# One attention and mixture-of-experts kernel on one core: VectorE's small work moved between its masking operations, both engines on the even unit's copy, value projections moved into the first two row tiles

## The reference

```python
xn = layernorm(x)
q, k, v = (xn @ W).reshape(4096, 2, 64)  for Wq, Wk, Wv
scores = einsum('nhd,mhd->hnm', q / 8, k)          # 2 heads, 4096 x 4096 each
scores = where(adj > 0, scores, -9e15)
attn = softmax(scores, axis=-1)
sat = einsum('hnm,mhd->nhd', attn, v).reshape(4096, 128)
y = concat([sat[:2048] @ weightr, sat[2048:] @ weightd]) + bias
x = x + leaky_relu(y, 0.01)
z = layernorm(x)
# 8 experts, top 2 chosen by gate scores; the mask is 0 or 1
h = gelu(einsum('td,edh->teh', z, W1) + b1)        # 256 hidden values each
x = x + sum over the chosen experts of (h @ W2 + b2)
```

## Time and profile before

| what | value |
|---|---|
| median of 3 runs | 851.81 us |
| profiled execution: time, and its span | 851.31 us, 849.5 us |
| PE busy | 811.7 us, 96% of the span |
| ACT busy | 679.0 us, 80% |
| DVE busy | 639.2 us, 75% |
| POOL busy | 195.5 us, 23% |
| chain that ended last | PE 73%, POOL 14%, issue 8%, DVE 3% |
| preparation, until the first scores | 0 to 41.2 us |
| step 0 and 1, until step 2's first transposes | 41.2 to 74.3 us |
| step 2 to the last scores | 74.3 to 633.7 us |
| last transposes and products, until the experts start | 633.7 to 657.5 us |
| feed-forward | 657.5 to 849.5 us |

### The profile page before, as it was taken

One profiled execution on the slowest core, in us unless ns is written; L12 is line 12 of the kernel. 1 busy time (PEld: TensorE's weight loads), 2 busy tenths in 40 slices (PEclk: granted clock), 3 DMA queues, 4 the chain that ended last, 5 costly groups with the idle time before them and its releaser, 6 DMA issues.

```text
span 849.5 us, 31821 instructions
## 1 busy us (share of the span) xinstructions
PE 811.7 (96%) x12080; PEld 597.7 (70%) x12080; DVE 639.2 (75%) x1530; ACT 679.0 (80%) x1099; POOL 195.5 (23%) x209
## 2 busy tenths in 40 slices
PE   4969999999999999999999999999997889999997
PEld 2537777777777777777777777777776567777775
DVE  6597888888888888888888888887883465555555
ACT  4838887878788888878888888788885789999996
POOL 4180000100100010000001000000000566766774
PEclk9979999999999999999999999999999999999999
DMA  8515433443343334434333443443100000000000
GB/s 220 110 25 91 81 58 58 66 74 58 56 77 59 56 61 72 65 56 69 67 56 58 68 71 56 63 72 56 31 0 2 1 14 14 14 14 12 12 12 12
DMA packets 40900, 44.96 MB, mean 53 GB/s; under 512 B 22168, under 2 KB 32160, under 8 KB 40864
## 3 DMA queue, kind: packets, MB, share of 16 engines
q0 software_dynamic: 9216, 33.56, 24.6%
q1 hardware_dynamic: 31216, 10.71, 5.4%
q10 hardware_dynamic: 432, 0.20, 0.1%
HBM read 71.72 MB, written 2.10 MB: 87 GB/s over the span
## 4 chain that ended last, share of the span: by engine, by line
PE 73%; POOL 14%; issue 8%; DVE 3%; DMA 1%; ACT 0%; POOLq 0%; DVEq 0%
PE ps L912 28%; PE ps L881 19%; PE ps L896 19%; POOL prob L349 14%; PE ps L923 2%; PE ps L837 1%; PE ps L842 1%; PE ps L850 1%; DVE prob L589 1%; PE ps L931 1%; PE ps L828 1%; DMA x_sb<-in_x 1%; DVE stats L513 0%; POOLq L348 0%; ACT prob L418 0%
## 5 line engine op out<-in xcount | busy, mean ns | idle before, releaser
L589 DVE CUSTOM_DVE_ANT_0 prob<-ps,mask 128x1024 f32<-128x1024 f32 x256 | 311.8, 1219 | 90.1 <-PE ps L881 84.4
L418 ACT ACTIVATE prob<-prob,nmax 128x1024 f32<-128x1024 f32 x256 | 292.8, 1144 | 9.9 <-DVE nmax L597 9.9
L912 PE MATMUL ps<-pt,v_sb 128*64 128x128 f32 x4096 | 253.2, 277 | 0.0
L912 PEld LDWEIGHTS ps<-pt,v_sb 128*64 128x64 f32 x4096 | 222.4, 137 | 13.4 <-issue 7.5
L433 ACT ACTIVATE pt<-ps 128x1024 f32<-128x1024 f32 x128 | 131.1, 1024 | 113.0 <-PE ps L896 113.0
L896 PEld LDWEIGHTS ps<-ident,prob 64*128 64x128 f32 x4096 | 152.6, 139 | 78.5 <-issue 78.4
L881 PE MATMUL ps<-k_half,q_row 64*128 64x512 f16 x1536 | 189.7, 380 | 5.0 <-DVE low L589 5.0
L896 PE MATMUL ps<-ident,prob 64*128 64x64 f32 x4096 | 183.7, 229 | 9.4 <-issue 4.7
L349 POOL TENSOR_TENSOR prob<-prob 128x512 f16<-128x512 f32 x104 | 122.6, 1183 | 57.1 <-ACT prob L483 54.4
L294 POOL DMA_DIRECT2D mask<-in_adj x64 | 35.4, 553 | 429.2 <-DVE low L589 429.2
L791 DVE SCALAR_TENSOR_TENSOR x_sb<-ps,k_half,x_sb 128x128 f32 (+1 forms) x256 | 72.5, 344 | 78.1 <-PE ps L1029 76.8
(11 more groups left out here) (97 smaller groups left out, 670.8 us busy)
## 6 DMA issues: line engine op xcount, KB each, us to landing
mask<-in_adj POOLq DMA_DIRECT2D x64, 512.0 KB, 5.5
q_row<-q_nat SPq DMA_DIRECT2D x128, 32.0 KB, 4.7
x_sb<-in_x SPq DMA_DIRECT2D x4, 512.0 KB, 7.0
out<-x_sb SPq DMA_DIRECT2D x8, 256.0 KB, 2.3
pt<-in_L_ffn_W SPq DMA_DIRECT2D x1, 1024.0 KB, 6.5
wq_sb<-in_L_gnn_Wq ACTq DMA_DIRECT2D x1, 64.0 KB, 2.9
wk_sb<-in_L_gnn_Wk ACTq DMA_DIRECT2D x1, 64.0 KB, 4.5
wv_sb<-in_L_gnn_Wv ACTq DMA_DIRECT2D x1, 64.0 KB, 5.7
```

The costliest lines, as they stand in the source:

```text
L418: act.activation(prob[:, h, cols], prob[:, h, cols], ACT.Exp, bias=nmax[:, h:h + 1], scale=-1.0, accum_out=sums[:, j, h, p:p + 1]).then_in ...
L589: dve.tensor_tensor_reduce(out=prob[:, h, col_of(p)], in0=ps[:, 2 * (u % 2):2 * (u % 2) + 2, :].rearrange("p b c -> p (b c)"), in1=mask[:, ...
L912: ins = pe.matmul(ps[dims, AV, 0:P], v_sb[:, tile, dims], pt[:, UNITS.index((h, p)), t, :], start=(tile == 0), stop=(tile == NT - 1))
```

## The change

It has these parts:

- **Copies:** ACT and DVE now empty one bank each for the even units (2k), and ACT alone empties both for the odd units (2k+1). `copies_by_dve` counts accordingly.
- **DVE's order:** small work that stood behind the odd mask of a quarter now stands between the even mask and the odd mask; `finish_tile` goes ahead of unit 2's copy; `residual` moves from the odd step into the next even one; `keep_logits` into the next odd step. The odd mask now waits for the transposes by itself (it stood behind the copy that did).
- **PE's order:** `x2_transpose` and `logits` go behind the quarter's `attend`.
- **Value projections:** all eight leave the preparation. Five run in step 0, between its scores, three in step 1. `xn_t` is no ring any more: it holds all eight chunks in units 4 to 7 of `pt`. The expert weights are loaded into `x2t_hi` and `x2t_lo` instead of there.
- **POOL's order:** the loads of `adj` for tiles 2 and 3 now come ahead of the splitting of the weights, which no longer waits for `k_lo_ready`.
- **Tail:** `rank_gates` moves from ahead of the last step into it, behind unit 2's copy. Steps 4 and 5 are now written out too.

```diff
-        w1_raw = pt[:, 4:6, :, :].rearrange("p u k q -> p (u k q)")
-        w2_raw = pt[:, 6:8, :, :].rearrange("p u k q -> p (u k q)")
+        w1_raw = x2t_hi[:, :].bitcast(F32)
+        w2_raw = x2t_lo[:, :].bitcast(F32)
...
-        xn_t = area(0, 4, 4).rearrange("p (r c) -> p r c", r=4)
+        xn_t = pt[:, 4:NU, :, :].rearrange("p u k q -> p (u k q)").rearrange("p (j c) -> p j c", j=NC)
...
-            return NU // 2 * j + units // 2
+            return NU // 2 * j + (units + 1) // 2
...
             load_adj(1, 1)
-            pool.wait_ge(k_lo_ready, NC)
+            load_adj(2, 0)
+            load_adj(3, 1)
             pool.wait_ge(w1_in, 16)
             split_weights(0, w1_raw, w1_pair)
...
-            for i in range(2, 6):
-                load_adj(i, i % 2)
+            load_adj(4, 0)
+            load_adj(5, 1)
...
-                copy_v(2 * p)
-                copy_v(2 * p + 1)
...
+            for j in range(V_FIRST):
+                copy_v(j)
...
-                if u % 2:
+                if u % 2 == 0:
                     act.activation(pt[:, u, :, 0:DH], ps[:, TR0, :].rearrange("p (k q) -> p k q", k=KT),
                                    ACT.Copy).then_inc(pt_by_act, 1)
...
+                    if early and u in (1, 3, 5):
+                        copy_v(V_FIRST + u // 2)
...
+                if u % 2 and prior:
+                    dve.wait_ge(transposed, NU * i - NU + u + 1)
...
                 for u in range(NU):
-                    if prior and u % 2:
+                    if finish and u == 2:
+                        finish_tile(i - 2, par)
+                    if prior and u % 2 == 0:
                         copy_pt(i - 1, u, early)
                     if now:
-                        mask_scores(i, par, u)
+                        mask_scores(i, par, u, prior)
                         if u in (5, 7):
                             row_max(i, u // 7, u)
-                    if u == 1 and finish:
-                        finish_tile(i - 2, par)
-                    if ahead and u in (3, 7):
+                    if ahead and u in (2, 6):
                         make_mask(i + 1, 1 - par, u // 4)
                     if post and par == 1:
-                        if u == 1:
+                        if u == 0 and ready:
+                            keep_logits(i - 5)
+                        if u == 0:
                             invert_sums(i - 3)
-                        if u == 3:
+                        if u == 4:
                             divide(i - 3)
-                        if u == 5:
+                        if u == 6:
                             leaky(i - 3)
-                        if u == 7:
-                            residual(i - 3)
                     if post and par == 0:
-                        if u == 1:
+                        if u == 0:
+                            residual(i - 4)
                             statistics(i - 4)
-                        if u == 3:
+                        if u == 4:
                             normalise(i - 4)
-                        if u == 5:
+                        if u == 6:
                             x2t_low(i - 4)
-                        if u == 7:
-                            keep_logits(i - 4)
+                    if last and u == 2:
+                        rank_gates(0, 0, RANKED_EARLY)
...
-            rank_gates(0, 0, RANKED_EARLY)
-            step(NT, 0, now=False, ahead=False)
+            step(NT, 0, now=False, ahead=False, last=True)
...
-                project_v(2 * p)
-                project_v(2 * p + 1)
...
+                    if not prior:
+                        project_v(k)
+                    if not prior and k == 3:
+                        project_v(k + 1)
                     if prior:
                         transposes(i - 1, 2 * k + 1, early)
+                    if early and k < NC - V_FIRST:
+                        project_v(V_FIRST + k)
```

More of the change, by code:

```diff
@@ L51 @@
 DVE_LOWS = (2, 4, 6)
+V_FIRST = 5
 def build(nc, x, adj, wq, wk, wv, wr, wd, bias, wg, bg, w1, b1, w2, b2, out):
@@ L460, in _ @@
             step(3)
-            pairs(act, 4, NT, lambda i, par: step(i, post=par == 0))
+            step(4, post=True)
+            step(5)
+            pairs(act, 6, NT, lambda i, par: step(i, post=par == 0))
             step(NT, now=False, post=True, last=True)
```

49 lines of the change are left out of this document (24 added, 25 removed).

## The result

| | before | after |
|---|---|---|
| median | 851.88 us (851.72 to 853.3) | 856.77 us (6 runs, 854.3 to 858.61) |
| profiled execution, its span | 851.31, 849.5 us | 858.61, 855.6 us |
| first scores | 41.22 | 39.24 |
| first transposes of step 1, 2, 3 | 53.36, 74.33, 92.01 | 53.98, 74.93, 95.23 |
| from step 3's first transposes to step 32's | 541.7 | 544.0 |

The ratio is 1.0051, with a 95% interval of 1.0034 to 1.0067. The prediction was 844.0, with a range of 839.8 to 849.3, and faster: both wrong. By the spans the changed kernel loses 3.2 us ahead of step 3, 2.3 in the 29 steps that the prediction had 5.7 us shorter, and 2.0 in the feed-forward, and gains 1.4 in the tail: 6.1. The profiled execution of the changed kernel was the slowest of its six, 1.8 us over the median; by the medians the loss is 4.9 us.

The account below looks back on a forecast made before the run. PE was taken as the bound, busy for 96% of the span. Start 0.4 lost, loop 5.7 and tail 2.5 gained: -7.8 from 851.31 gives 843.5, plus 0.5 for the median, 844.0 us; range 839.8 to 849.3.

Parts of the forecast that it names:

- Copies of the even unit: Loop, steps 3 to 31: sharing the copy frees the banks before PE needs them, 0.08 us at most per quarter, 8.7 gained.
- DVE's order: Loop: DVE's copy comes late in one quarter of eight, by 0.21 us, 14.5 times, 3.0 us lost.
- small work W: DVE's small operations between even and odd mask: up to about 1.3 + 0.2 us fits, as in seven of eight quarters.
- Slower, VectorE late everywhere: Rival, chance 0.05: in every quarter the even copy waits behind mask, small work and mask; loop 13.9 us more, 863.
- Preparation: Before the first scores: three rounds gain 0.85 us each, the last about 0.4; first scores at 38.3 instead of 41.22.
- Step 0: First scores to step 1: 14.5 us instead of 12.1, so step 1 starts at 52.8 instead of 53.36.
- Steps 1 and 2, and the weight split: Step 1 takes 19.0 us, step 2 starts at 71.8, PE waits for POOL's split before step 3; 0.4 us lost.
- the 93.2: Predicted start of step 3 in us with a half-clock stretch; 91.5 without it.
- Tail: Last step until the experts: 23.8 us falls to 20.4, or 22.1 with a half-clock stretch; middle taken, 2.5 gained.

Follow-up runs that it names:

- the pair of kernels with the loop written out: The kernel before, and it with only the copies changed, each with DVE's loop over steps 4 to 29 written out: 852.3 and 846.8 us.
- the kernel with the loop written out: The changed kernel with DVE's loop over steps 6 to 29 written out step by step, other engines' loops kept: 845.1 us, ratio 0.9916.
- the early split: The changed kernel with POOL's weight split moved ahead of the loads of adj for tiles 2 and 3: 862.8 us, ratio 1.0124.
- the spread split: The changed kernel, value projections in the preparation, DVE's loop written out, and the weight split taken forward in two parts around tile 3's second half load: 840.4 us.

## Why the prediction was wrong, by its steps

*Copies of the even unit*: the mechanism was right, 1.84 us from even to odd transposes wherever DVE is in time. That the pair of kernels with the loop written out gives 8.8 us against the 8.7 counted is luck. Added up over the 116 quarters of steps 3 to 31, the distances from even to odd transposes went from 222.5 to 219.0 us, 3.6 us, as one quarter in eight is still late there (2.20). The other 5.2 us lie in the distances from odd to the next even transposes, 319.3 to 314.0, which the prediction held fixed: behind a quarter in time it is 2.49 instead of 2.54 us.

*DVE's order* is the step that failed. It gave one late quarter of 0.21 us in two steps, 3.0 us in all. Three were late: by 2.07, 2.30 and 2.32 less 1.84 each, 1.17 us in two steps, 14 us over the 12 turns alone. Over steps 3 to 31 the even-to-odd distances stand 15.0 us above 1.84 each, where before they stood 9.0 above it (all that the copies could gain there, counted as 8.7), and the odd-to-even ones are 3.7 us shorter: 15.0 - 9.0 - 3.7 = 2.3, the loop's loss.

The count of small work W took the operations and left out what stands between them: 0.32 us behind divide (W was 1.57, from 332.39 to 333.96, not 1.3), 0.17 behind leaky, and the 0.47 us of the jump; residual with statistics took 1.78 (341.88 to 343.66) and not 1.65. The waits and the jump are not seen in the rows that I read, since before, DVE waited for scores behind each. Without the loop the same order has late quarters of 0.09 and 0.30, 0.39 in two steps, still more than the 0.21 told, and its loop is 541.7 - 534.3 = 7.4 us shorter than before, inside the 2.8 to 8.7 that the prediction allowed.

The rival *Slower, VectorE late everywhere* had the mechanism and not the place: DVE was late in three quarters of eight, not in all. Its 1.18 us is also a slip: by the prediction's own terms a copy started at 1.92 - 0.79 = 1.13 gives back the loop's gain, and at 1.15 the tail's too.

*Preparation*: 39.24 against 38.3, and the 38.3 was right in sum and not in its parts. The rounds took 5.62 instead of 6.4 us as told, but only two of them. The first took 9.24 us against 8.39 before, as the full clock began at 20.02 and not at 18.34; in the kernel with the loop written out, whose preparation is the same, the clock rose at 18.42, the round took 8.40, so that there was nothing to gain in it, and the first scores came at 38.49. The last part, to the first scores, gained 1.2 us instead of the 0.4 counted.

*Step 0*: its end was 1.2 us later than told, 0.9 of it from the preparation; by itself it took 14.7 against 14.5. The copies of v stand ahead of the first exponential as predicted, and PE waits 1.90 us for it.

*Steps 1 and 2, and the weight split*: step 2 came 3.1 us late, and POOL's split with it. The term of 0.4 us lost was 3.2. The step that fails is the 19.0 us for step 1, which took 21.0 (74.93 - 53.98), with the clock at half for 3.4 us. Its first quarter took 5.3 us and not 3.85, the second 5.9 and not 5.4. The half clock had been priced, at 1.7 us, and gave the 93.2, but the sum took a value between. The last 2.0 us to 95.23 are 1.2 from the preparation and step 0, 0.2 in step 1, and 0.6 more from step 2's start to step 3's (20.3, told as 19.7). The order of things (PE waits for POOL, "a step 3 that starts after 95" would speak against it) was named, with 95.23 at its edge. The experiments put the loss on the projections in steps 0 and 1, for without them everything comes 5.1 us earlier.

The question that the prediction left open, whether make_mask is held by POOL's operations with one input too, is answered by the early split, for a normalisation of x in place of make_mask: one that began at 22.63 lasted 1.92 us beside L306 (22.53 to 24.46), the next 2.06 beside L308 (24.55 to 26.45). The rule cited there held: the Trainium skill, page "SBUF — State Buffer", section "Who interferes with whom", says that whichever engine starts first has the shared ports for its whole instruction. The rows agree for L310 too: make_mask took 2.67 and 3.96 us and ended 0.6 us behind it.

*Tail*: 22.4 us, 1.4 of the 2.5 gained. The ranking held unit 4's copy by 1.27 us (begun at 649.72, ACT's of the other bank at 648.45), against the 1.5 told. The prediction gave 20.4 us without a stretch at the half clock and 22.1 with one. Here 3.4 us were at half, from 651.49; the three kernels whose tail has no such stretch took 20.7 to 20.9 us. So the term was right within 0.5 us once the clock is known. The 0.3 to 0.5 left are in part the even-to-odd distance, 1.71 us where 1.54 was told.

On the jump the Trainium skill has a figure that I did not use, page "Advanced Engine Details and Errata", section "Control Flow Timing": a compare-and-branch of about 108 ns. The stop measured here is 0.47 us, 0.51 by the turns taken away, over four times as long; by the page's figure the twelve turns would have cost 1.3 us (an estimate), and by the turns taken away they cost 6.2. The measurement decides; which instructions make up the stop no row shows.

## What to carry to other kernels

When work is moved to a place without slack, count not only its instructions but the stops between them: waits of an engine for its own results, and the jump of its loop. The trace of before hides them wherever the engine then waits for another, so read them as start minus the end before, in a stretch where it doesn't wait. Put a wait ahead of the consumer and not behind the producer, and let a loop turn where its engine has slack; here the one was worth 10.7 us and the other 5.2, each by itself, with hardly a line changed.

## What was not expected of the hardware

- DVE's jump back costs 0.47 us in its timeline, 0.51 us per turn by the difference of six turns. On an engine that waits there anyway no cost is measured (852.3 against 851.6 us, a ratio of 1.0004).
- In the loop a mask begins 0.32 us behind the result of divide that DVE waits for, and 0.17 us behind it with the same steps written out; behind leaky it is 0.17 us in both.
- A split on POOL stretches DVE's operations wherever it stands: 0.69 us to 2.50, 2.67 and 3.96 for make_mask, 0.34 to between 1.92 and 4.07 for the normalisation. Of the places tried in the changed kernel the latest was the best; with the projections in the preparation it and the spread split can't be told apart.
